# Start of a gated cross-attention and FFN kernel: loads reordered, Wq split by output columns, constant matmuls ahead of q, and new instruction orders

## The chip, the cores and the metric

The kernel runs on one core of one Trainium2 chip. The time is device microseconds of one launch, and the lower one is better. The names of the engines are those of the profile: PE is TensorE (matmul), PEld its weight load, DVE is VectorE, ACT ScalarE, POOL GpSimd, SP SyncE. SPq and ACTq in a row are the queues that issue DMAs.

## What is computed

A transformer layer over 8 batches of 256 tokens of width 512, with grouped cross-attention (32 query heads of 16, 8 key/value groups) and a gated FFN of width 1536:

```python
def xattn(X, enc, causal_mask, padding_mask, Wq, bq, Wk, bk, Wv, bv, Wo, bo):
    q, k, v = X @ Wq.T + bq, enc @ Wk.T + bk, enc @ Wv.T + bv
    # 8 groups, 4 query heads to a group, head size 16
    scores = einsum('bgrqd,bgkd->bgrqk', q, k) / sqrt(16)
    scores = where(causal_mask, -inf, scores); scores = where(padding_mask, -inf, scores)
    out = einsum('bgrqk,bgkd->bgrqd', softmax(scores), v)
    return out @ Wo.T + bo
def ffn(x, gate_w, up_w, down_w, gate_scale, up_scale, down_scale):   # weights rounded to fp8 e4m3
    return ((silu((x @ gate_w8) * gate_scale) * ((x @ up_w8) * up_scale)) @ down_w8) * down_scale
x = x + tanh(g_xattn) * xattn(layernorm(x), ctx_2048, ...)
x = x + tanh(g_ffn) * ffn(layernorm(x), ...)
```

## The kernel before

There is no loop over tiles. The work is cut into pieces with a name, a number n and a batch b, and five strings of words (PE_ORDER, ACT_ORDER, DVE_ORDER, POOL_ORDER, SP_ORDER) give the order of the pieces on each engine. `order()` turns a string into a list; the n-th word of a name is its n-th piece. Each engine walks through its list (the loops `for name, n, b in ..._ORDER`) and issues what belongs to the piece, with its semaphore waits, so a piece whose wait is not met holds up everything behind it on its engine. The strings were written out in advance; nothing is chosen at run time.

The pieces of one batch, in the order of the data:

- `load_x`, `stats1`, `power_0`, `shift1`, `norm1`: x comes in (`xin`), mean and variance on DVE, the power on POOL, the normalization on ACT (`xn`).
- `xT`: two pieces of four transposes on PE into a work bank; ACT copies the high half to f16 (`xh`) and DVE makes the rest (`xl`). Every product of activations is made of three f16 matmuls (high by high, high by low, low by high), so each weight has a high and a low part too.
- `q` (two pieces of 24 matmuls of 128x256), `k` (12) and `v` (24 of 128x128). `cT` makes the two f16 parts of the context on ACT and POOL (`ch`, `cl`).
- `put_q`, `get_q`, `put_k`, `get_k`: q and k go to DRAM and come back with the heads spread over the partitions (`qs`, `ks`). Each get is six DMAs.
- `maxima`: 16 pieces. PE makes the scores of four heads (4 matmuls), DVE takes the row maxima with the mask `mq` added (L741, four instructions of 0.42 us each, started 0.34 us apart). After eight of them `mrow` transposes the maxima, ACT and POOL split them, and `rows` writes them into `qs` as two more rows.
- `scores`: 16 pieces. For the first batch PE adds the mask by a matmul (`mask_b`, `ident_b`) and ACT exponentiates from the bank (`exp`); for later batches DVE adds the mask (L750).
- `weighted`, `sums`, `den`, `gather`, `recip`, `spread`, `split_att`, `out`: the weighted sum of v, its denominator, and the output projection.
- `norm2`, `x2T`, `gu` (12 pieces of 16 matmuls), `fuse`, `fsplit`, `down_a`, `down_b`, `add_y`, `store`: the FFN.

The weights are set up once. Each comes in as float32 into a buffer that is used for something else later (Wq into `un`, Wo into `ws`, Wk and Wv into `att_u`), ACT makes the high part and DVE the low part. This is the `setup` piece; SETUP names them in a fixed order, and the waits (`set_high`, `set_free`) count them in that order. The FFN weights come as 12 slabs of 768 KB through two staging buffers (`f_h`, `f_l`); the piece `slab` on SP issues the load and the piece `slab` on ACT waits for it and casts it to fp8 (L599). PE has three work banks, each given to the pieces in turn, and two pairs of banks for scores.

The first loads stand ahead of the lists. SP issues x, Wq (1 MB), ctx, Wo (1 MB), two masks, bv, two gates, spread, bo, the down scale and the padding rows; ACT issues ident, Wk, the columns of biases and scales, the padding columns and Wv.

## Time and profile before

| | us |
|---|---|
| median of 3 runs | 613.05 |
| the three runs | 613.05, 614.70, 609.72 |
| the profiled execution | 617.89 |
| its span, first to last instruction | 616.1 |
| PE busy | 563.3 (91%) |
| DVE busy | 485.9 (79%) |
| ACT busy | 363.7 (59%) |
| POOL busy | 255.8 (42%) |

The profiled execution took 1.8 us more than its span and 4.8 us more than the median. The page divides the span into 40 slices of 15.4 us and gives the busy tenths of each engine; the rows of a timeline give the start and the length of instructions, and in brackets how long the engine had been idle and what ended that.

### The profile page before, as it was taken

How to read it: one execution, taken by the hardware profiler on the slowest of the kernel's cores; microseconds unless marked ns; L12 is line 12 of the kernel's file. 1: busy time of each engine (PE TensorE's matmuls, PEld its weight loads, DVE VectorE, ACT ScalarE, POOL GpSimd, SP SyncE). 2: the span in 40 equal slices, each digit the busy share in tenths (PEclk: the TensorE clock that was granted, in tenths of full speed). 3: DMA queues.
4: the chain of work that ended last, by engine and by line, in shares of the span. 5: the costliest groups of instructions: out<-in, count | busy, mean ns of one | idle time of the engine just before them, and what ended most of it. 6: DMA issues, size and time to landing. Idle time of an engine off the chain costs nothing.

```text
span 616.1 us, 14167 instructions
## 1 busy us (share of the span) xinstructions
PE 563.3 (91%) x5056; PEld 348.4 (57%) x5056; DVE 485.9 (79%) x1505; ACT 363.7 (59%) x668; POOL 255.8 (42%) x339
## 2 busy tenths in 40 slices
PE   0846888799999999999999999999998999799997
PEld 0633343357754775467745765476645764376683
DVE  2377768999899889988999999988998898744321
ACT  3533675787754765556665576576644764475261
POOL 4043041123552078424464166306711464248274
PEclk9956999699999999999999999999997999799999
DMA  8662465571222033211322412112203000101000
GB/s 299 221 210 85 106 200 113 121 267 37 80 60 73 14 83 111 58 50 40 102 83 70 112 37 81 44 31 66 73 3 95 2 28 29 53 3 53 1 36 34
DMA packets 57158, 50.30 MB, mean 82 GB/s; under 512 B 8000, under 2 KB 46976, under 8 KB 57088
## 3 DMA queue, kind: packets, MB, share of 16 engines
q1 hardware_dynamic: 55600, 48.79, 26.9%
q8 instruction: 40, 0.66, 0.5%
q10 hardware_dynamic: 1488, 0.61, 0.4%
q14 instruction: 30, 0.25, 0.1%
HBM read 35.21 MB, written 9.44 MB: 72 GB/s over the span
## 4 chain that ended last, share of the span: by engine, by line
PE 73%; DVE 13%; issue 8%; POOL 2%; ACT 2%; DMA 1%; POOLq 0%; SPq 0%; DVEq 0%
PE work L982 25%; PE work L993 12%; PE av L890 8%; PE work L921 7%; PE work L960 5%; DVE junk L741 5%; PE sc L862 5%; PE sc L880 4%; DVE ws L750 2%; PE work L931 2%; DMA cin<-in_ctx_t 1%; PE work L907 1%; PE work L941 1%; PE sc L876 1%; PE work L969 1%
## 5 line engine op out<-in xcount | busy, mean ns | idle before, releaser
L741 DVE CUSTOM_DVE_ANT_0 junk<-sc,mq 128x256 bf16<-128x256 f32 x496 | 180.0, 418 | 26.5 <-PE sc L862 26.0
L750 DVE SCALAR_TENSOR_TENSOR ws<-sc,padc,mask_k 128x1024 f32<-128x1024 f32 x112 | 143.3, 1279 | 19.4 <-PE sc L880 18.0
L614 ACT ACTIVATE ws<-ws 128x1024 f32<-128x1024 f32 x112 | 116.8, 1053 | 19.7 <-DVE ws L750 19.4
L538 POOL TENSOR_TENSOR ff<-ga,up 128x256 f32<-128x256 f32 x96 | 69.3, 729 | 120.7 <-DVE ga L826 117.0
L982 PE MATMUL work<-h_h,wg 128*128 128x256 f16 x384 | 90.4, 276 | 0.0
L982 PE MATMUL work<-h_l,wg 128*128 128x256 f16 x384 | 89.8, 274 | 0.0
L982 PE MATMUL work<-h_h,wu 128*128 128x256 f16 x384 | 89.4, 273 | 0.0
L982 PE MATMUL work<-h_l,wu 128*128 128x256 f16 x384 | 89.3, 273 | 0.0
L674 ACT ACTIVATE up<-work,fuse_s 128x256 f32<-128x256 f32 x96 | 45.2, 471 | 55.5 <-PE work L982 55.5
L993 PE MATMUL work<-wd,f_h 128*128 128x512 fp8e4 x192 | 73.0, 380 | 0.1
L993 PE MATMUL work<-wd,f_l 128*128 128x512 fp8e4 x192 | 72.8, 379 | 0.0
L890 PE MATMUL av<-ws,va 128*32 128x256 f32 x1024 | 71.3, 397 | 1.5 <-ACT un L620 0.9
L545 POOL TENSOR_TENSOR f_l<-ff,f_h 128x256 f16<-128x256 f32 x96 | 63.5, 674 | 19.0 <-ACT f_h L682 18.9
L862 PE MATMUL sc<-ks,qs 48*128 48x256 f16 x512 | 52.5, 283 | 14.8 <-DVE mx L741 14.6
L826 DVE SCALAR_TENSOR_TENSOR ga<-th,work 128x256 f32<-128x256 f32 x96 | 38.8, 415 | 24.6 <-ACT th L675 24.3
L880 PE MATMUL sc<-qs,ks 50*128 50x256 f16 x512 | 51.7, 278 | 4.9 <-DVE ws L750 4.9
L620 ACT ACTIVATE un<-av 128x256 f32<-128x256 f32 x64 | 24.4, 381 | 48.5 <-PE av L890 48.1
L682 ACT ACTIVATE f_h<-ff 128x256 f16<-128x256 f32 x96 | 38.5, 416 | 21.1 <-POOL ff L538 21.0
L982 PEld LDWEIGHTS work<-h_h,wg 128*128 128x128 fp8e4 x384 | 37.6, 98 | 19.3 <-issue 15.0
L675 ACT ACTIVATE th<-work,tanh_s 128x256 f32<-128x256 f32 x96 | 45.1, 469 | 0.0
L890 PEld LDWEIGHTS av<-ws,va 128*32 128x32 f32 x1024 | 27.4, 111 | 29.6 <-issue 17.1
L741 DVE DVE_READ_ACCUMULATOR2_ANT mx<- 128x1 f32 x512 | 42.0, 82 | 0.0
(116 smaller groups left out, 1013.6 us busy)
## 6 DMA issues: line engine op xcount, KB each, us to landing
qs<-q_scratch SPq DMA_DIRECT2D x96, 64.0 KB, 2.4
xin<-in_x SPq DMA_DIRECT2D x8, 512.0 KB, 4.6
cin<-in_ctx_t SPq DMA_DIRECT2D x8, 512.0 KB, 4.5
xb<-in_x SPq DMA_DIRECT2D x8, 512.0 KB, 4.7
att_u<-un SPq DMA_DIRECT2D x128, 32.0 KB, 2.0
out_x<-yt SPq DMA_DIRECT2D x16, 256.0 KB, 2.2
ks<-k_scratch SPq DMA_DIRECT2D x48, 64.0 KB, 2.4
q_scratch<-qh SPq DMA_DIRECT2D x16, 128.0 KB, 2.5
```

Source lines behind the costliest of these rows:

```text
L538: pool.tensor_tensor(ff[:, n % RING, :], ga[:, n % RING, :], up[:, n % RING, :], ALU.mult).then_inc(ff_done, 1)
L545: pool.tensor_tensor(f_l[:, n, :], ff[:, n % RING, :], f_h[:, n, :], ALU.subtract).then_inc(fl_ready, 1)
L614: act.activation(ws[:, unit, :, :], ws[:, unit, :, :], ACT.Exp, scale=1.0 / SSC).then_inc(exp_done, 1)
L674: act.activation(up[:, n % RING, :], bank[:, L:2 * L], ACT.Copy, scale=fuse_s[:, n:n + 1])
L675: act.activation(th[:, n % RING, :], bank[:, 0:L], ACT.Tanh, scale=tanh_s[:, n:n + 1]).then_inc(tanh_done, 1)
L741: last = dve.tensor_tensor_reduce((junk, junk_1)[maxima_banks(n, b)][:, j, :], sc[maxima_banks(n, b)][:, place(j)], mq[b % 2][:, t, :], 1. ...
L750: dve.scalar_tensor_tensor(out=ws[:, n % 4, :, :], in0=sc[1][:, :].rearrange("p (j l) -> p j l", j=HPG), scalar=padc[b % 2][:, kt:kt + 1], ...
L862: last = mm(sc[maxima_banks(n, b)][:, place(j)], qs[b % 2][at:at + 3 * HD, pair, t * P:(t + 1) * P], ks[b % 2][at:at + 3 * HD, g, :], star ...
L880: last = mm(sc[1][:, place(j)], ks[b % 2][at:at + 3 * HD + 2, g, kt * P:(kt + 1) * P], qs[b % 2][at:at + 3 * HD + 2, pair, :], start=b >= ...
L890: last = mm(av[32 * j:32 * (j + 1), 0:L], va[b % 2][:, kt, n, :], ws[:, 2 * (n % 2) + kt, 2 * (j % 2) + j // 2, :], start=kt == 0, stop=kt ...
L982: last = mm(bank[:, L * i:L * (i + 1)], w[:, k, n * P:(n + 1) * P], d[:, k, :], start=k == 0 and s == 0, stop=k == KT - 1 and s == 1)
L993: last = mm(bank[:, :], d[:, c, n * P:(n + 1) * P], wd8[:, c, :], start=c == 0 and s == 0, stop=c == FT - 1 and s == 1)
```

## The change

1. Loads. x of the first batch is loaded in two halves, one from SP's queue and one from ACT's. Wq is loaded and set up by halves of its output columns (`wq_columns`) instead of halves of its input rows. Wo and the small loads go later on SP's queue, the padding rows earlier; Wk goes behind the padding columns on ACT's queue.
2. Setup. The words of the order strings name the weight, and each setup piece has its own semaphores, so they may stand in any order. The first `q` piece waits for `Wq0` alone, the second for `Wq1`.
3. The first `get_k` (batch 0) is issued by ACT instead of SP (`k_by_act=1`).
4. `warm`: 20 matmuls of 128x512 f16 on a constant tile into the bank `av`, 17 ahead of the first transposes and 3 behind them. They wait for one memset on DVE and nothing reads them.
5. `mask_b` is a piece of its own on POOL.
6. All five order strings are new.

```diff
-def order(words, setup=(), by_pe=0):
+def order(words, by_pe=0, k_by_act=0):
...
-            if name == "setup":
-                pieces.append((name, setup[k], 0))
+            if name in SETUP:
+                pieces.append(("setup", SETUP.index(name), 0))
...
 PE_ORDER = order("""
-    k xT*2 q*2 v xT*2 maxima*3 q maxima*6 mrow q maxima k maxima scores maxima scores xT maxima scores weighted
+    warm*17 xT*2 warm*3 q k q v xT*2 maxima*2 q maxima*2 q maxima k maxima*4 mrow v xT maxima*2 scores maxima scores
...
 ACT_ORDER = order("""
-    setup cT*2 setup*2 norm1 k xT*2 q setup*2 slab*2 gates setup q norm1 xT*2 cT q cT slab mrow norm1 q k exp*3 slab
+    slab Wk norm1 Wq0 xT*2 cT Wq1 cT q Wo0 k Wv gates q get_k norm1 xT*2 cT*2 slab norm1 slab q*2 Wo1 mrow k exp*2
...
 DVE_ORDER = order("""
-    setup stats1 setup shift1 setup*2 k xT*2 q setup v stats1 setup*2 q gates shift1 setup xT*2 maxima*8 q stats1
-    maxima shift1 maxima k maxima q maxima*4 v maxima xT maxima xT maxima*4 q maxima*3 stats1 maxima*2 shift1 q
+    stats1 shift1 Wq0 xT*2 mask columns Wk Wq1 q k stats1 gates shift1 Wo0 q Wv v xT*2 maxima*2 stats1 maxima shift1
+    maxima*5 q*2 maxima Wo1 k maxima*3 v maxima xT maxima*3 xT maxima*3 q maxima*4 stats1 maxima q maxima*3 k shift1
...
 SP_ORDER = order("""
-    load_c slab*2 load_x put_k put_q get_k get_q slab load_x put_q slab get_q slab put_q rows get_q put_k load_c
+    slab load_x slab put_q put_k load_c get_q load_x slab load_xb put_q get_q put_q rows put_k get_q load_c slab*2
...
+        def wq_columns(half):
+            return slice(2 * P * half, 2 * P * (half + 1))
...
+        def get_k(eng, b):
+            eng.wait_ge(k_out, 32 * (b + 1))
+            past(eng, t_ready, 16 * (b - 1))
+            if b < 2:
+                eng.wait_ge(sm_rows, 2)
+            for hf in range(2):
+                for s in range(3):
+                    src = k_dram[(0, 0, 1)[s]].rearrange("(g d) n -> d g n", d=HD)
+                    eng.dma_start(ks[b % 2][64 * hf + HD * s:64 * hf + HD * (s + 1), :, :], src).then_inc(ks_in, 16)
...
-            sp.dma_start(xin[:, :, :], x_v[0]).then_inc(ld_x, 16)
-            sp.dma_start(st_q[:, :, :], Wq_t.rearrange("(t p) i -> p t i", p=P)).then_inc(ld_wq, 16)
+            sp.dma_start(xin[:, 0, :], x_v[0][:, 0, :]).then_inc(ld_x, 16)
+            sp.dma_start(st_q[:, :, wq_columns(0)], wq_v[:, :, wq_columns(0)]).then_inc(ld_wq[0], 16)
             sp.dma_start(cin[:, :, :], c_v[0]).then_inc(ld_c, 16)
-            sp.dma_start(st_o[:, :, :], Wo_t.rearrange("(t p) i -> p t i", p=P)).then_inc(ld_wo, 16)
+            sp.dma_start(st_q[:, :, wq_columns(1)], wq_v[:, :, wq_columns(1)]).then_inc(ld_wq[1], 16)
...
+            act.dma_start(xin[:, 1, :], x_v[0][:, 1, :]).then_inc(ld_x, 16)
...
+            dve.memset(warm_in[:, :], 1.0).then_inc(warm_set, 1)
...
+            pe.wait_ge(warm_set, 1)
             for name, n, b in PE_ORDER:
+                if name == "warm":
+                    mm(av[:, :], warm_in[:, 0:P], warm_in[:, :], start=True, stop=True)
...
-                    if b == 0 and n == 0:
-                        pe.wait_ge(set_free, SETUP.index("Wq1") + 1)
+                    if b == 0:
+                        pe.wait_ge(set_free[f"Wq{n}"], 1)
```

On ACT, from its last first load on, before (in the names, `wk_h` and `wq_h` are the high parts of weights, `ch` that of the context, `xn` the normalized x, `wg` the fp8 gate weights):

```order
L590 ACT_TABLE_LOAD
L590 ACTIVATE wk_h<-att_u 128x512 [waits ld_wk]
L648 ACTIVATE ch<-cin 128x512 [waits ld_c] x2
L590 ACTIVATE wq_h<-un 128x1024 [waits ld_wq] x2
L626 ACTIVATE xn<-xin,nb,rs 128x512 [waits shift1]
L626 ACTIVATE xn<-xin,nb,rs 128x512
L654 ACTIVATE kh<-work,bk_c 128x256 [waits bank_ready0,columns_ready]
```

and now:

```order
L612 ACT_TABLE_LOAD
L612 ACTIVATE wg<-f_h 128x1536 [waits ld_f0]
L601 ACTIVATE wk_h<-att_u 128x512 [waits ld_wk]
L642 ACTIVATE xn<-xin,nb,rs 128x512 [waits shift1]
L642 ACTIVATE xn<-xin,nb,rs 128x512
L601 ACTIVATE wq_h<-un 128x4x256 [waits ld_wq0]
L653 ACTIVATE xh<-work 128x512 [waits bank_ready0]
L653 ACTIVATE xh<-work 128x512 [waits bank_ready1]
L666 ACTIVATE ch<-cin 128x512 [waits ld_c]
L601 ACTIVATE wq_h<-un 128x4x256 [waits ld_wq1]
L666 ACTIVATE ch<-cin 128x512 [waits ld_c]
```

The cast of the first slab, which stood behind the first q, is ACT's first piece, and the context and the second half of Wq stand behind the transposes.

On SP, the end of the first loads and what follows, before:

```order
L421 DMA dsb<-in_L_ffn_down_scale 128x512
L422 DMA padr_u<-in_mask_BxS_bk 128x2048
L438 DMA cin<-in_ctx_t 128x4x256 [waits c_low]
L432 DMA f_h<-in_L_ffn_gate_w 128x1536
L432 DMA f_l<-in_L_ffn_gate_w 128x1536
L435 DMA xin<-in_x 128x2x512 [waits normed1]
L461 DMA k_scratch<-kh 128x256 [waits bank_free0]
L461 DMA k_scratch<-kl 128x256
L447 DMA q_scratch<-qh 128x2x256 [waits bank_free0]
L447 DMA q_scratch<-ql 128x2x256
L470 DMA ks<-k_scratch 16x8x256 [waits sm_rows,k_out]
```

and now:

```order
L439 DMA dsb<-in_L_ffn_down_scale 128x512
L449 DMA f_h<-in_L_ffn_gate_w 128x1536
L452 DMA xin<-in_x 128x2x512 [waits normed1]
L449 DMA f_l<-in_L_ffn_gate_w 128x1536
L464 DMA q_scratch<-qh 128x2x256 [waits bank_free2]
L464 DMA q_scratch<-ql 128x2x256
L478 DMA k_scratch<-kh 128x256 [waits bank_free0]
L478 DMA k_scratch<-kl 128x256
L455 DMA cin<-in_ctx_t 128x4x256 [waits c_low]
L472 DMA qs<-q_scratch 16x8x256 [waits q_out0]
```

The first slab's load is the first issue behind the constants, the loads of ctx and of the second slab stand behind a wait, and `get_k` is gone from here.

On DVE, from the first `q` piece to the first maxima of the first batch, before:

```order
L772 SCALAR_TENSOR_TENSOR ql<-work,bq_c,qh 128x256 [waits q_high]
L772 SCALAR_TENSOR_TENSOR ql<-work,bq_c,qh 128x256
L718 SCALAR_TENSOR_TENSOR wv_l<-att_u,wv_h 128x512 [waits set_high]
L788 SCALAR_TENSOR_TENSOR va<-work,bv_b 128x8x16 [waits ld_bv,consts_pool,bank_ready2]
L788 SCALAR_TENSOR_TENSOR va<-work,bv_b 128x8x16
L688 BN_STATS bst<-xin 128x6 [waits ld_x]
L688 BN_STATS bst<-xin 128x6
L693 BN_AGGR mv<-bst 128x2 [waits stats1]
L693 BN_AGGR mv<-bst 128x2
L696 TENSOR_SCALAR ve<-mv 128x2 [waits bnagg1]
L702 TENSOR_SCALAR mask_q<-th 128x512 [waits ld_mask]
```

and now:

```order
L791 SCALAR_TENSOR_TENSOR ql<-work,bq_c,qh 128x256 [waits q_high]
L791 SCALAR_TENSOR_TENSOR ql<-work,bq_c,qh 128x256
L797 SCALAR_TENSOR_TENSOR kl<-work,bk_c,kh 128x256 [waits k_high]
L706 BN_STATS bst<-xin 128x6 [waits ld_x]
L706 BN_STATS bst<-xin 128x6
L711 BN_AGGR mv<-bst 128x2 [waits stats1]
L711 BN_AGGR mv<-bst 128x2
L714 TENSOR_SCALAR ve<-mv 128x2 [waits bnagg1]
L747 TENSOR_SCALAR tgbo<-tgbo,tg 128x512 [waits tanh_g]
L748 TENSOR_SCALAR tgo<-tg 128x1
L749 TENSOR_SCALAR dsb<-dsb,tg 128x512
L781 SCALAR_TENSOR_TENSOR nb<-mv,rs 128x2 [waits rstd1]
L736 SCALAR_TENSOR_TENSOR wo_l<-ws,wo_h 128x1024 [waits high_Wo0]
L791 SCALAR_TENSOR_TENSOR ql<-work,bq_c,qh 128x256 [waits q_high]
L791 SCALAR_TENSOR_TENSOR ql<-work,bq_c,qh 128x256
L736 SCALAR_TENSOR_TENSOR wv_l<-att_u,wv_h 128x512 [waits high_Wv]
```

The statistics of the second batch and, with them, the gates and `Wo0` stand ahead of the second q's low part, and `Wv`, which v waits for, stands behind it.

## Rows read from the trace of the kernel before

**Rows 1.** The page: the span in 40 slices of 15.4 us.

```profile
PE   0846888799999999999999999999998999799997
...
PEclk9956999699999999999999999999997999799999
```

**Rows 2.** Windows: stretch, its us, busy us by engine, granted clock, DMA share, GB/s.

```profile
3.00:14.00 11.00, 0.00 (x0) 0.00 (x0) 2.83 (x12) 4.94 (x6) 4.21 (x5) 1.00 1.05 358
...
40.00:63.90 23.90, 16.98 (x108) 9.51 (x104) 18.22 (x93) 6.71 (x12) 6.56 (x10) 0.65 0.41 138
63.90:100.00 36.10, 31.37 (x328) 15.05 (x332) 26.01 (x131) 26.72 (x36) 9.28 (x11) 1.00 0.50 137
100.00:121.80 21.80, 17.25 (x167) 8.09 (x166) 20.27 (x65) 13.61 (x19) 2.40 (x3) 0.77 0.57 127
...
520.00:540.00 20.00, 16.57 (x128) 8.15 (x126) 15.25 (x22) 10.02 (x17) 3.83 (x4) 0.83 0.14 41
```

**Rows 3.** Timeline of SP: start, duration, instruction.

```profile
11.21 0.43 SPq L422 DMA_DIRECT2D padr_u<-in_mask_BxS_bk  x1
...
28.31 2.80 SPq L470 DMA_DIRECT2D ks<-k_scratch  x6
```

**Rows 4.** DMA issues of 10 to 14.9 us: KB, us from issue to landing.

```profile
f_h<-in_L_ffn_gate_w SPq DMA_DIRECT2D x1, 768.0 KB, 7.3
...
padr_u<-in_mask_BxS_bk SPq DMA_DIRECT2D x1, 256.0 KB, 5.6
```

**Rows 5.** DMA issues of 46 to 60 us.

```profile
f_h<-in_L_ffn_up_w SPq DMA_DIRECT2D x1, 768.0 KB, 4.2
```

**Rows 6.** Timeline of ACT: start, duration, instruction, idle before and what ended it.

```profile
6.63 0.63 ACT L590 ACTIVATE wk_h<-att_u 128x512 f16<-128x512 f32 x1 [1.69 <-DMA att_u<-in_Wk_t]
...
14.90 1.52 ACT L626 ACTIVATE xn<-xin,nb,rs 128x512 f32<-128x512 f32 x2 [0.90 <-DVE nb L762]
...
18.62 0.60 ACT L637 ACTIVATE xh<-work 128x512 f16<-128x512 f32 x1 [0.26 <-PE work L907]
...
27.71 1.48 ACT L599 ACTIVATE wg<-f_h 128x1536 fp8e4<-128x1536 f32 x1
```

**Rows 7.** Timeline of PE, start of the program.

```profile
20.20 0.37 PE L921 MATMUL work<-xh,wq_h 128*128 128x256 f16 x1 [1.62 <-DVE xl L766]
...
26.49 0.27 PE L921 MATMUL work<-xl,wq_h 128*128 128x256 f16 x1
26.60 0.27 PE L921 MATMUL work<-xh,wq_l 128*128 128x256 f16 x1
...
37.39 1.97 PE L907 MATMUL work<-ident,xn 128*128 128x128 f32 x8 [7.54 <-ACT xn L626]
```

**Rows 8.** The chain that ended last, in order of time: start, us, what.

```profile
28.51 1.35 PE work L941 x24
...
55.51 5.03 PE work L921 x24
```

**Rows 9.** DMA issues of 27 to 31 us.

```profile
ks<-k_scratch SPq DMA_DIRECT2D x6, 64.0 KB, 2.5
...
q_scratch<-ql SPq DMA_DIRECT2D x1, 128.0 KB, 2.0
```

**Rows 10.** Timeline of DVE: setup work and maxima of the first batch.

```profile
14.79 2.35 DVE L718 SCALAR_TENSOR_TENSOR wq_l<-un,wq_h 128x1024 f16<-128x1024 f32 x2
...
30.30 1.27 DVE L688 BATCH_NORM_STATS2 bst<-xin 128x6 f32<-128x512 f32 x2
...
40.63 0.41 DVE L741 CUSTOM_DVE_ANT_0 junk<-sc,mq 128x256 bf16<-128x256 f32 x1
...
47.89 0.42 DVE L741 CUSTOM_DVE_ANT_0 x<-sc,mq 128x256 bf16<-128x256 f32 x1 [3.04 <-PE sc L862]
...
54.78 0.87 DVE L772 SCALAR_TENSOR_TENSOR ql<-work,bq_c,qh 128x256 f16<-128x256 f32 x2
```

**Rows 11.** Timeline of ACT, first exponential of the first batch.

```profile
63.92 1.11 ACT L610 ACTIVATE ws<-sc,padc 128x1024 f32<-128x1024 f32 x1 [1.12 <-PE sc L880]
```

More of the change, by code:

```diff
@@ new lines @@
+    weighted maxima scores maxima weighted x2T*2 maxima scores q maxima scores weighted gu maxima scores gu*2 scores
+    maxima k gu weighted maxima scores gu mrow gu scores maxima gu weighted scores maxima gu scores gu maxima scores
+    gu weighted maxima scores v gu scores maxima weighted gu down_a maxima scores down_a spread maxima scores
+    weighted spread down_b xT maxima scores xT down_b maxima scores mrow out maxima out weighted maxima scores q
+    scores weighted x2T maxima scores x2T q scores maxima weighted gu*2 maxima scores gu maxima gu scores maxima
@@ new lines @@
+    weighted gu*2 maxima scores mrow gu*2 k scores maxima weighted gu scores maxima gu weighted scores maxima gu
+    scores v gu scores weighted down_a scores maxima down_a spread scores maxima down_b spread maxima weighted xT
+    scores maxima down_b mrow xT maxima scores out*2 scores weighted maxima q maxima weighted scores x2T maxima x2T
+    q scores weighted maxima gu scores gu maxima scores gu*2 maxima scores gu weighted maxima scores gu mrow maxima
+    gu*2 weighted scores maxima gu k scores gu scores weighted maxima scores gu maxima weighted scores v gu maxima
@@ new lines @@
+    scores down_a spread down_a maxima scores spread down_b xT maxima scores weighted xT maxima down_b mrow maxima
+    scores out*2 weighted scores maxima q maxima weighted x2T*2 maxima scores q maxima gu scores gu scores maxima
+    weighted gu maxima scores k gu maxima scores weighted gu mrow maxima scores gu*2 scores maxima weighted gu*2
+    scores maxima v weighted scores gu scores maxima gu scores gu maxima scores weighted down_a maxima down_a spread
+    scores maxima down_b spread weighted maxima scores down_b mrow maxima scores out maxima out weighted xT scores
@@ new lines @@
+    maxima xT weighted scores k maxima x2T*2 q*2 maxima scores gu*2 maxima scores weighted gu maxima scores gu
+    maxima weighted scores gu mrow maxima scores gu weighted scores maxima gu*2 scores maxima gu weighted scores
+    maxima gu*2 maxima scores down_a gu maxima scores weighted down_a scores maxima spread down_b maxima scores
+    weighted spread down_b maxima scores mrow out scores out weighted maxima scores weighted v scores maxima x2T*2
+    maxima weighted scores gu maxima gu scores maxima gu scores gu maxima scores gu weighted maxima gu mrow scores
@@ L154 @@
     gu*12 down*2
[L155 removed]
+""", by_pe=BY_PE)
 POOL_ORDER = order("""
[L157 to L170 removed]
@@ L182 @@
+    load_xb rows load_c get_q put_q den gather put_k store get_k rows store load_x put_q load_c get_q load_xb gather
+    rows den put_q store get_q put_k gather get_k rows get_q put_k rows gather put_q load_xb den store get_q gather
+    store get_k rows load_xb gather put_q get_q rows store den store gather rows load_xb store gather den store
+    gather store*4
+""", k_by_act=1)
 IN_BANKS = ("xT", "q", "k", "v", "spread", "out", "x2T", "gu")
@@ L589, in _ @@
                     act.wait_ge(loaded, 16)
-                    act.activation(w_h, stage, ACT.Copy, scale=scale).then_inc(set_high, 1)
+                    act.activation(w_h, stage, ACT.Copy, scale=scale).then_inc(set_high[SETUP[n]], 1)
+                if name == "get_k":
+                    get_k(act, b)
                 if name == "gates":
@@ L616, in _ @@
                 if name == "sums":
+                    if n == 0 and b == 0:
+                        act.wait_ge(set_free["Wq1"], 1)
                     act.wait_ge(av_ready, AV_USE["weighted", n, b] + 1)
```

226 lines of the change are left out of this document (101 added, 125 removed).

## Prediction

> **What bounds the kernel now.** I read the slices first. PE shows 9 almost everywhere after the first tenth of the span, and the low digits lie in the first five slices, where PEclk is low too [rows 1]. So the long middle is bound by PE, an order with the same matmuls can win little there, and this change has to earn its time in the first 64 us. The windows put a size on it: from 40 to 63.9 us PE is busy 16.98 of 23.9 us at a mean clock of 0.65, and DVE 18.22; from 63.9 to 100 PE is busy 31.37 of 36.1 and DVE 26.01; from 100 to 121.8 DVE is busy 20.27 of 21.8 and PE 17.25, at 0.77 [rows 2]. Up to 100 us neither engine is full, they hand work to each other; then DVE binds until the FFN of the first batch gives PE its filler.
>
> The start is a chain: x, norm, xT, q, through DRAM and back, maxima. The reader should see four points of it: the transposes' second high part on ACT at 18.62 [rows 6], q at 20.20 [rows 7], the first maxima on DVE at 40.63 and the eighth's end at 54.78, where the next instruction begins [rows 10], the first exponential at 63.92 [rows 11]. These are what I compute anew.
>
> **The loads and the first piece of ACT.** ACT's list now begins with the cast of slab 0, ahead of Wk, norm1, Wq0 and xT. ACT works in order, so the whole start waits for that load. When does it land? SP reached the end of its first loads at 11.21 + 0.43 = 11.64 [rows 3]; one issue more (x in halves, Wq in halves, against one each, less one that ACT takes) makes about 12.1 for slab 0. The amount ahead of it is the same as before, and in that time the DMA engines were full: share 1.05, 358 GB/s from 3 to 14 us [rows 2]. The last of these loads landed at 11.21 + 5.6 = 16.8 [rows 3, 4]. Behind it 0.786 MB at 358 GB/s take 2.2 us: 19.0. The other way: slab 0 of the kernel before took 7.3 us from issue to landing in the same crowd [rows 4]: 12.1 + 7.3 = 19.4. Bounds: a slab in a quiet stretch took 4.2 us [rows 5], so 16.3 at the earliest; if the queue moves it only after everything and lands it a microsecond later, 20.5. I take L = 19.4. Before, ACT's first activation ran at 6.63 and norm1 at 14.90 [rows 6].
>
> **From L to the first maxima.** ACT: slab 1.4 (1.48 less the overlap that all rows show, 0.1), Wk 0.5, norm1 1.5 [rows 6]: the transposes begin at L+3.5. Before, eight transposes at the low clock kept PE 1.97 us [rows 7]. The second high part starts 1.9 us in, L+5.4; q started 1.6 us after that instruction (18.62 to 20.20) [rows 6, 7]: q at L+7.0. Wq0's low part (1.2 us, half of 2.35 [rows 10]) fits in between on DVE.
>
> The 17 constant matmuls are over by some 8 us and PE then has nothing until L+3.5 = 22.9. In this trace the clock was at its low level again after the 7.54 us without work ahead of 37.39 (eight transposes 1.97 us; the slices show it) [rows 1, 7]. So these 17 buy nothing; the three behind the transposes keep PE occupied for 1.3 us while it would wait. q began at 20.20 at the low clock, and only at 26.2 did the matmuls come 0.11 us apart (26.49, 26.60) [rows 7]; I let it rise as late in the unbroken stretch as there, 6.0 us, at L+9.5. Twelve matmuls at 0.21 (5.03 us for 24 [rows 8]) and twelve at 0.11: q ends at L+10.8. k (12 matmuls, 1.3) ends at L+12.1 and the second q (2.6) at L+14.7; Wk's and Wq1's low parts are ready at L+8.6 and L+9.7.
>
> The way out and back: the high part of q 0.9, low part 0.9, two puts issued by L+13.6, the second landing 2.0 after its issue at L+13.1 [rows 9], get_q 2.8 of issue (six ks copies took 2.80 [rows 3]) and 2.5 from the last issue to landing: L+20.1. k's parts reach DRAM at L+15.7; ACT issues get_k from there to L+18.5, in place by L+20.7. Here the change moves 2.8 us from SP onto ACT, and what is queued behind it on ACT is norm1 of batch 1, for which PE's list puts xT ahead of the maxima. Before, both gets stood one behind the other on SP, so the move saves up to 2.8 us there; with norm1 behind it, it gives back most: norm1 ends at L+20.1.
> The Trainium skill, DMA: Bandwidth & Descriptors, section "Issuing engines are not separate DMA queues", says that issuing on two engines saves only sequencer time, usually small beside the DMA. By that rule this part would be worth nothing, and the time 2.8 us later at most. The rows here speak against "small": 2.80 us of issue beside 2.5 to land [rows 3, 9].
>
> DVE in that stretch does stats1 (1.7 with the aggregate; 1.27 for the two statistics [rows 10]), gates 1.1, Wo0 1.2, the second q's low part 0.9 and only then Wv, at L+19.0; v, and so PE, waits for it from L+14.7. After 4.3 us idle I let the clock fall. v 2.6 at the low clock (1.35 at the full one [rows 8]), xT 1.97: the second high part at L+23.5, its low part 0.6 later, and the maxima on DVE another 0.6 later, L+24.8 = 44.2. With the clock kept it would be L+22.7. Before: 40.63. **The first maxima come 3.6 us later.**
>
> **From the maxima to the first exponential.** Before, eight maxima took 54.78 - 40.63 = 14.15 us for 8 x 1.38 = 11.0 of work; 3.04 was one wait for PE, which ran a whole q at the low clock between the third and the fourth [rows 10]. Now a q stands behind the second and one behind the fourth maxima, and stats1 (1.7) on DVE covers the first of them. If PE is at full clock by then (it has been busy since L+19.0), neither q (2.6) makes DVE wait: 11.0 + 1.8 = 12.8, and I take 13.2 for handovers. The eighth ends at 57.4, 2.6 later than before. Behind it DVE has both q low parts (1.6), one maxima (1.38), Wo1 (1.2), k (0.4), one maxima (1.38), 6.0 in all, and the eleventh maxima starts about 63.7 with the exponential 0.8 behind it: 64.5. Before: 63.92. The rows for the scores leave 2.8 us of issue and about 2 of landing after the split maxima, 64 as well, so they are level with it.
>
> So the start is nearly even in time: +0.6. But by then PE has done v of batch 1 and one xT of batch 2 beforehand, which stood behind the first scores: 1.35 [rows 8] and about 0.5. Against that, DVE had only one q low part (0.87, [rows 10]) more to do before. If PE binds the next stretch, the gain is 1.85 - 0.6 = 1.25; if DVE does, 0.87 - 0.6 = 0.3. Neither binds alone up to 100 us [rows 2]. I take 0.8.
>
> **The rest.** mask_b as a piece of its own, the per-weight semaphores and the column halves add no instruction in a place where someone waits; the work is the same. I find the same number of matmuls ahead of the first gu piece and of each later batch's in both lists, to within 2 us of work. The two dips of the middle and the end (520 to 540 us: PE busy 16.57 of 20, clock 0.83 [rows 2]) lie where batches change, and the new list has the same neighbours there. Nothing, with 3 us either way in the range.
>
> **Sum.** 616.1 - 0.8 = 615.3 for the span, 617.1 for a profiled execution with its 1.8 us around; that of before lay 4.8 over the median, so the median is forecast at 613.05 - 0.8 = 612.25, **612.2 us**, no change that a measurement can tell (1% of this kernel is 6.1 us, and its three runs spread over 5).
>
> **Rivals.** (a) The slab lands early, at 16.3. All points move 3.1 us forward: 609.1. For it: ACT's share of the loads leaves by its own queue. Against: 7.3 and 5.6 us in the rows of that stretch [rows 4].
> (b) The clock stays up from the constant matmuls, or rises at the third xT and stays. Then q(0) saves 1.2, and v and xT 2.1 on the path: about 609. Against: the idle 7.54 us and the low clock after it [rows 1, 7]. The Trainium skill, TensorE: Matmul & The Clock Gate, section "Why this matters for your kernels", advises to keep TensorE busy continuously to reach the full clock; it is the premise of the warm pieces, and by it alone they would pay.
> (c) The start isn't made up. If PE runs the two q pieces at the low clock (5.03 each [rows 8]), DVE waits 1.3 and 2.3 as it waited 3.04 [rows 10]; the distance from first maxima to first exponential stays 23.3 and the exponential comes at 67.5, 3.6 late: 616.6. It decides if PE's clock isn't up when the first q stands between maxima. If the later DVE-bound stretch then loses the clock once more than now (21.8 us with 17.25 busy at 0.77 [rows 2] is such a stretch, some 4 us lost), 621.
> (d) The new lists differ from the old ones in the long middle by chance: one of the later dips gone is 3.4 us, both 6.8: 605 to 609 with the forecast's start.
>
> **Chances.** Forecast 0.41 (own range 609 to 616), (a) and (b) together 0.22, of which a third with some of (d) below 607; (c) 0.23, of which 0.15 reaches 619; (d) 0.14. Below 606.9 lie 0.07 + 0.14 = 0.21, above 619.2 some 0.17, and 0.62 between. Range: 604 to 620.
>
> **What the profile after will show.** ACT's first activation is the slab cast, at about 19.4; if it is at 16, (a). Norm1 at 21.3, q at 26.4, first maxima on DVE at 44, first exponential at 64. The constant matmuls end by 9 us and PE is idle until 23. The forecast is wrong if ACT begins before 15 us, or if the middle (121 to 600 us) loses or gains over 3 us of PE time.

## The result and the profile after

The changed kernel took 620.94 us (median of 4 runs, 620.21 to 622.97), the kernel before 612.66 (4 runs, 609.72 to 614.70). The ratio is 1.0149, 95% interval 1.0116 to 1.0182: slower by 1.5%, 8.3 us. The forecast was 612.2 and its range ended at 620.0.

The slices of the page, 40 of 15.5 us, answer to [rows 1]:

```profile
PE   3557798788999999999999999999999999899997
...
PEclk8588599779999999999999999999999999899999
```

The reader is to see PEclk: in seven of the first ten slices it is below 9, against three before, and of the two late dips one is left, at 8 instead of 7. The first slices have to be read beside the matmuls, though: in the trace before, the column has 1.00 from 14 to 26 us, while the matmuls of 128x256 came 0.21 us apart from 14.16 to 26.1, the distance that they have in stretches with 0.50; so the low level lasted there until 26.1. PE's busy digits hardly tell the difference, since slow matmuls count as busy. The windows of the same stretches as [rows 2], with two more (14 to 26 and 58.7 to 75.8); the columns are the stretch, its length, the busy us of PE, PEld, DVE, ACT and POOL, the granted clock, the DMA share and GB/s:

```profile
3.00:14.00 11.00, 3.60 (x14) 1.33 (x12) 1.86 (x6) 1.28 (x1) 2.66 (x3) 0.86 1.08 355
14.00:26.00 12.00, 3.22 (x11) 2.01 (x11) 2.46 (x4) 6.27 (x9) 0.13 (x1) 0.50 0.51 181
40.00:63.90 23.90, 18.09 (x146) 13.08 (x144) 19.45 (x88) 10.17 (x17) 6.77 (x10) 0.79 0.52 136
58.70:75.80 17.10, 13.20 (x74) 5.77 (x74) 12.28 (x56) 4.83 (x7) 0.66 (x1) 0.50 0.55 183
63.90:100.00 36.10, 30.46 (x264) 12.15 (x260) 23.83 (x120) 21.85 (x29) 4.28 (x4) 0.83 0.54 173
100.00:121.80 21.80, 17.31 (x175) 8.19 (x174) 19.02 (x71) 13.99 (x18) 2.62 (x4) 0.84 0.18 46
520.00:540.00 20.00, 17.31 (x140) 7.17 (x133) 16.38 (x36) 11.55 (x17) 3.75 (x4) 0.92 0.18 55
```

From 14 to 26 us, where the kernel before ran k, transposed x and began q (PE busy 10.22 us in the same window of its trace), PE is busy 3.22 of 12 us. The row of 58.7 to 75.8 has a granted clock of 0.50, the lower of the two levels (1.2 GHz), for 17.1 us; in the trace before the same window has 0.95. The timeline of ACT answers to [rows 6]:

```profile
4.01 1.28 ACT L612 ACT_TABLE_LOAD   x1 [4.01 <-issue]
19.15 1.48 ACT L612 ACTIVATE wg<-f_h 128x1536 fp8e4<-128x1536 f32 x1 [13.86 <-DMA f_h<-in_L_ffn_gate_w]
20.54 0.61 ACT L601 ACTIVATE wk_h<-att_u 128x512 f16<-128x512 f32 x1
21.06 1.50 ACT L642 ACTIVATE xn<-xin,nb,rs 128x512 f32<-128x512 f32 x2
...
24.68 0.60 ACT L653 ACTIVATE xh<-work 128x512 f16<-128x512 f32 x1 [0.26 <-PE work L929]
...
36.01 2.76 ACTq L418 DMA_DIRECT2D ks<-k_scratch  x6
38.87 1.52 ACT L642 ACTIVATE xn<-xin,nb,rs 128x512 f32<-128x512 f32 x2 [3.99 <-issue]
...
68.10 1.11 ACT L624 ACTIVATE ws<-sc,padc 128x1024 f32<-128x1024 f32 x1 [7.22 <-PE sc L900]
```

ACT has nothing from 5.29 to 19.15: it waits for the load of slab 0 (`f_h`). Behind that stand the casts, norm1 at 21.06 and the second high part of xT at 24.68 (before 18.62). The timeline of SP and the DMA issues of 3 to 20 us say when that load was issued and how long it was on its way, as [rows 3] and [rows 4]:

```profile
9.12 0.43 SPq L439 DMA_DIRECT2D dsb<-in_L_ffn_down_scale  x1
9.74 0.33 SPq L449 DMA_DIRECT2D f_h<-in_L_ffn_gate_w  x1
```

```profile
f_h<-in_L_ffn_gate_w SPq DMA_DIRECT2D x1, 768.0 KB, 9.4
...
padr_u<-in_mask_BxS_bk SPq DMA_DIRECT2D x1, 256.0 KB, 8.2
```

Issued at 9.74, landed 9.4 us later: 19.1. The timeline of PE, as [rows 7]:

```profile
1.44 5.16 PE L872 MATMUL av<-warm_in 128*128 128x512 f16 x17 [1.44 <-DVE warm_in L739]
22.70 1.94 PE L929 MATMUL work<-ident,xn 128*128 128x128 f32 x8 [16.11 <-ACT xn L642]
24.44 1.49 PE L872 MATMUL av<-warm_in 128*128 128x512 f16 x3
26.15 0.37 PE L943 MATMUL work<-xh,wq_h 128*128 128x256 f16 x1 [0.23 <-DVE xl L785]
...
28.14 0.27 PE L943 MATMUL work<-xl,wq_h 128*128 128x256 f16 x1
...
38.17 0.23 PE L963 MATMUL work<-wv_h,ch 128*128 128x128 f16 x1 [4.22 <-DVE wv_l L736]
...
44.49 0.61 PE L882 MATMUL sc<-ks,qs 48*128 48x256 f16 x8 [2.30 <-DMA ks<-k_scratch]
...
69.27 1.03 PE L896 MATMUL sc<-mask_b,ident_b 128*128 128x512 bf16 x2 [0.52 <-ACT ws L624]
```

The 17 constant matmuls end at 6.6, and then PE waits 16.11 us. q starts at 26.15 at the low clock (0.21 us apart until 28.02, then 0.11). v waits 4.22 us for Wv's low part, the first maxima 2.30 us for `ks`. The DMA issues of 34 to 40 us have the gets, against [rows 9]:

```profile
cin<-in_ctx_t SPq DMA_DIRECT2D x1, 512.0 KB, 4.5
qs<-q_scratch SPq DMA_DIRECT2D x6, 64.0 KB, 5.1
ks<-k_scratch ACTq DMA_DIRECT2D x6, 64.0 KB, 5.8
```

The gets, issued side by side by SP and ACT, took 5.1 and 5.8 us from issue to landing, where `ks` took 2.5 before. 512 KB of ctx are issued just ahead, but that doesn't explain it alone: with both gets on SP and the same ctx ahead of them they took 3.1 and 2.8 us (below). The timeline of DVE, as [rows 10]:

```profile
25.92 1.40 DVE L720 TENSOR_SCALAR mask_q<-th 128x512 f32<-128x512 uint8 x1
...
27.57 1.12 DVE L725 TENSOR_SCALAR padc_all<-padc_u 128x16 f32<-128x16 uint8 x1
...
45.04 0.42 DVE L760 CUSTOM_DVE_ANT_0 junk<-sc,mq 128x256 bf16<-128x256 f32 x1 [1.39 <-PE sc L882]
...
47.80 1.28 DVE L706 BATCH_NORM_STATS2 bst<-xin 128x6 f32<-128x512 f32 x2
```

First maxima at 45.04 (before 40.63), first exponential at 68.10 (before 63.92, [rows 11]).

Both kernels were run and profiled a second time, and those two traces are the fairer pair, as told below. The legs between points of the program, in us (a batch's second norm is the first `x2n` row of that batch on ACT), each worked out as the difference of two starts:

| | before | before, 2nd | changed | changed, 2nd | slab later | combined |
|---|---|---|---|---|---|---|
| start to first maxima | 40.6 | 37.3 | 45.0 | 45.4 | 36.1 | 33.0 |
| to first exponential | 23.3 | 22.1 | 23.1 | 21.8 | 22.5 | 20.8 |
| to norm2 of batch 0 | 69.9 | 69.8 | 74.6 | 72.3 | 73.1 | 71.3 |
| to norm2 of batch 5 | 331.6 | 331.6 | 331.2 | 332.6 | 331.2 | 331.2 |
| to norm2 of batch 6 | 63.9 | 63.8 | 59.2 | 60.7 | 59.2 | 59.2 |
| to the end | 86.8 | 85.1 | 85.9 | 86.2 | 85.9 | 85.7 |
| span | 616.1 | 609.6 | 619.0 | 619.1 | 607.9 | 601.1 |

Second against second, the changed kernel loses 8.1 us up to the first maxima and 2.6 between exponential and norm2, and wins 3.0 between batches 5 and 6. The first trace of the kernel before is an unusual execution: of the 76 timed executions of that kernel on record here, 73 took 609.7 to 615.0 us and three took 617.7 to 617.9, this one among them.

### The profile page after: what moved, and what is told of

It is laid out like the page before. It is cut to its first block, busy times and chain, and to the rows that moved or that the text cites. A ratio compares the mean times of both kernels' runs of the same rounds, so it can differ in the third digit from the quotient of the medians.

```text
span 619.0 us, 14216 instructions
## 1 busy us (share of the span) xinstructions
PE 567.7 (92%) x5076; PEld 347.8 (56%) x5076; DVE 484.8 (78%) x1506; ACT 363.9 (59%) x668; POOL 255.8 (41%) x339
## 4 chain that ended last, share of the span: by engine, by line
PE 78%; DVE 9%; SPq 4%; DMA 4%; issue 2%; ACT 1%; ACTq 0%; POOLq 0%; POOL 0%; DVEq 0%
PE work L1005 28%; PE work L1016 12%; PE av L910 8%; PE work L983 7%; PE work L943 5%; PE sc L882 5%; PE sc L900 5%; DVE junk L760 4%; DMA ks<-k_scratch 2%; DMA f_h<-in_L_ffn_gate_w 2%; DVE ws L769 1%; PE work L963 1%; PE work L953 1%; PE sc L896 1%; PE work L929 1%
## 5 line engine op out<-in xcount | busy, mean ns | idle before, releaser
L769 DVE SCALAR_TENSOR_TENSOR ws<-sc,padc,mask_k 128x1024 f32<-128x1024 f32 x112 | 143.3, 1280 | 20.3 <-PE sc L900 17.9
L1005 PEld LDWEIGHTS work<-h_h,wg 128*128 128x128 fp8e4 x384 | 37.5, 98 | 19.1 <-issue 14.2
```

The costliest lines, as they stand in the source:

```text
L769: dve.scalar_tensor_tensor(out=ws[:, n % 4, :, :], in0=sc[1][:, :].rearrange("p (j l) -> p j l", j=HPG), scalar=padc[b % 2][:, kt:kt + 1], ...
L1005: last = mm(bank[:, L * i:L * (i + 1)], w[:, k, n * P:(n + 1) * P], d[:, k, :], start=k == 0 and s == 0, stop=k == KT - 1 and s == 1)
```

## The experiments

Ratios are to the kernel before, timed on the same chip beside each, with the 95% interval. Theory A: one word, the cast of slab 0 in first place on ACT, costs the time. The rivals put the loss on the new order further on, above all on PE at its low clock between the maxima, or on the constant matmuls.

**The slab's cast later.** The changed kernel with one word moved on ACT:

```diff
-    slab Wk norm1 Wq0 xT*2 cT Wq1 cT q Wo0 k Wv gates q get_k norm1
+    Wk norm1 Wq0 xT*2 cT Wq1 cT q Wo0 k Wv slab gates q get_k norm1
```

> The changed kernel with one word moved: the cast of slab 0 on ACT goes from the first place to behind Wv. Theory A (the 13.9 us for which ACT waits for slab 0 are what the start loses): ACT begins with Wk near 8 to 9 us, q at about 15 instead of 26.2, first maxima on DVE at 34 to 36 instead of 45.0, and the time falls by 8 to 11 us, to 610 to 613. Theory B (other waits, such as the late Wv and the low clock, take the place of the stall): q comes 10 us earlier, but the time falls by less than 4 us.

Measured: 610.10 us, ratio 0.9961 (0.9931 to 0.9991), 10.8 under the changed kernel (9.7 under its second set of runs, 619.83). With the word moved, the rest of the change is 2.1 us faster than the kernel before. The timeline of ACT in it:

```profile
10.82 0.63 ACT L601 ACTIVATE wk_h<-att_u 128x512 f16<-128x512 f32 x1 [5.51 <-DMA att_u<-in_Wk_t]
11.35 1.50 ACT L642 ACTIVATE xn<-xin,nb,rs 128x512 f32<-128x512 f32 x2
...
14.98 0.60 ACT L653 ACTIVATE xh<-work 128x512 f16<-128x512 f32 x1 [0.26 <-PE work L929]
```

norm1 starts at 11.35 instead of 21.06, 9.7 us sooner, and the median follows by 9.7 to 10.8. Now norm1 waits for Wk, whose load ends the idle time ahead of 10.82.

**The same word put into the kernel before.** Its slab cast goes first on ACT, its load ahead of ctx on SP:

```diff
-    setup cT*2 setup*2 norm1 k xT*2 q setup*2 slab*2 gates      (ACT)
+    slab setup cT*2 setup*2 norm1 k xT*2 q setup*2 slab gates
-    load_c slab*2 load_x put_k                                  (SP)
+    slab load_c slab load_x put_k
```

> The kernel before with the cast of slab 0 as ACT's first piece, and its load ahead of the second ctx on SP, nothing else. Theory A: ACT begins at 19 to 20 instead of 6.6 us, norm1 at 24 instead of 14.9, and the time rises by 9 to 12 us over the kernel before, so the stall alone costs more than the whole change. Theory B (there is slack elsewhere in the start): it rises by less than 5 us.

Measured: 623.67 us, ratio 1.0174 (1.0123 to 1.0225), 11.4 us over the kernel before beside it (612.23). The timeline of ACT in it:

```profile
20.14 1.48 ACT L599 ACTIVATE wg<-f_h 128x1536 fp8e4<-128x1536 f32 x1 [15.40 <-DMA f_h<-in_L_ffn_gate_w]
...
25.97 1.52 ACT L626 ACTIVATE xn<-xin,nb,rs 128x512 f32<-128x512 f32 x2 [0.89 <-DVE nb L762]
```

The cast waits 15.40 us for the same load, and the old order pays for it as the new one does. Two words were moved here, the cast and its load. So slab 0 in first place costs 10 to 11 us in either order.

**Without the constant matmuls,** the changed kernel with `warm*17` and `warm*3` taken out of PE's list:

> The changed kernel without its 20 constant matmuls. Theory A (PE is idle for 16 us between them and the transposes, so they buy nothing): within 1.5 us of the changed kernel, q at 26 us as before. Rival (the three behind the transposes bring the clock up early): q ends 1 to 2 us later and the time rises by as much.

Measured: 619.64 us, 1.0127 (1.0086 to 1.0168), q at 26.46 against 26.15. The medians differ by 1.3 us, in favour of the version without them, and the intervals overlap: they buy nothing here.

**The same, with the slab later:**

> The slab cast moved and the 20 constant matmuls ahead of q taken out. With the slab cast moved, PE is idle for 5.2 us between the 17 of them and the transposes. Theory (the matmuls pay once the stall is gone: q ran at full clock from 17.2 us on): 2 to 3 us slower than with them. Rival (q isn't what the start waits for): within 1 us.

Measured: 609.16 us, 0.9936 (0.9909 to 0.9963), 0.9 under the version with them. I expected them to be worth 2 to 3 us once the long wait was gone; they weren't, though q's matmuls, 0.11 us apart from 16.95 on with them, came 0.21 us apart up to 19.35 without.

**Constant matmuls put into the kernel before,** 28 ahead of k and 4 behind the first transposes:

```diff
-    k xT*2 q*2 v xT*2 maxima*3 q
+    warm*28 k xT*2 warm*4 q*2 v xT*2 maxima*3 q
```

> The kernel before with constant matmuls of 128x512 on PE, 28 ahead of k and 4 behind the first transposes, nothing else. In its two profiles the clock rose at 26.2 and at about 18 us, and the first maxima on DVE followed at 40.6 and 37.3. Theory (the time at which the clock rises varies between executions, and q at half clock costs the start 3 us): the clock is high before q in the profile, first maxima at 36 to 37.5, and the median falls by 0 to 2 us with less spread. Rival (it makes no difference to the median): within 0.5 us.

Measured: 611.30 us, 0.9977 (0.9954 to 1.0000). q ran at 19.42 at the full clock, first maxima at 36.94 as expected, and the median moved 1.2 us, at the edge of what can be told. The spread didn't shrink as I had expected (609.24 to 614.25, against 609.77 to 614.76), so the clock ahead of q is not what spreads the usual executions. Its trace is a control for the first one of the kernel before: all legs from the first maxima on are the same (23.3, 69.9, 331.6, 63.9, 86.8), and only the first is shorter, 36.9 instead of 40.6. So about 3.7 us of that trace are the low clock up to 26.2 us, in k, the transposes and q.

**Constant matmuls between the maxima.** The changed kernel with 18 more, which keep PE at work while it waits for DVE; `hold` waits until DVE has taken the eighth maxima and writes a score bank that is free then:

```diff
-    maxima k maxima*4 mrow v xT maxima*2 scores
+    maxima k maxima*2 warm*5 maxima warm*4 maxima warm*3 mrow v xT maxima hold*6 maxima scores
...
+                if name == "hold":
+                    pe.wait_ge(m_free, UNITS // 2)
+                    mm(sc[1][:, 0:D], warm_in[:, 0:P], warm_in[:, :], start=True, stop=True)
```

> The changed kernel with 18 more constant matmuls of 128x512, which stand where PE waits for DVE among the maxima of the first batch (5 before the eighth, 4 before the ninth, 3 before mrow, 6 before the eleventh, these into the second score bank). In the changed kernel the clock is low from 58.7 to 75.8 us. Theory C (that low stretch costs about 4 us of the start): the clock stays high there and the time falls by 3 to 5 us. Rival (DVE sets the pace there): the clock is high, the time within 1 us.

Measured: 619.06 us, 1.0114 (1.0068 to 1.0159). One window of it, to be held against the same window of the changed kernel above:

```profile
58.70:75.80 17.10, 12.68 (x114) 5.15 (x113) 15.10 (x72) 6.43 (x9) 0.67 (x1) 1.00 0.48 167
```

The clock stays at 1.00 instead of 0.50, and the leg from the exponential to norm2 is 70.2 us instead of 74.6. In the second trace of the changed kernel the same window has 0.62 and the leg is 72.3. In the median 1.9 us appear (0.8 against the second set of runs), where I had expected 3 to 5 and which is less than the intervals can separate.

**The same fill with the slab later:**

> The kernel with the slab cast moved, and with the 18 constant matmuls among the first maxima as well. The clock was low from 58.2 to 71.9 us with the slab cast moved alone. Theory C (the gaps that the new list leaves on PE ahead of mrow let the clock fall, and the first scores then run at half of it, whatever ACT waited for): 3 to 5 us less than the slab cast moved alone, 605 to 607. Rival: within 1 us of it.

Measured: 609.08 us, 0.9922 (0.9898 to 0.9946), 1.0 under the version without fill, where I had expected 3 to 5. Here the fill didn't hold the clock all the way: it was at 0.50 from about 61 to 68 us, against 58 to 71 without, and the leg from the exponential to norm2 is 71.6 us against 73.1.

**Wv's low part ahead of stats1 on DVE,** with the slab later:

```diff
-    Wk Wq1 q k stats1 gates shift1 Wo0 q Wv v
+    Wk Wq1 q k Wv stats1 gates shift1 Wo0 q v
```

> The slab cast moved, and on DVE the low part of Wv ahead of the second batch's statistics instead of behind the second q, so that PE doesn't wait 4.0 us for it ahead of v. Theory (that wait, and the clock that falls in it, is on the path): v and xT end 3 us earlier, but the first maxima wait for k from DRAM (2.2 us of that wait is seen), so the time falls by 0.5 to 2 us. Rival: the gain is 3 us or more, since the clock stays up.

Measured: 608.58 us, 0.9932 (0.9908 to 0.9957), 1.5 less than with the slab later alone. It did not hold up in the combined version (below).

**The first get_k back on SP,** with the slab later:

```diff
-    slab gates q get_k norm1                  (ACT)
+    slab gates q norm1
-    put_q put_k load_c get_q                  (SP)
+    put_q put_k load_c get_k get_q
```

> The slab cast moved and the first get_k issued by SP again, ahead of get_q. Theory (both gets one behind the other on SP cost 2.8 us, of which norm1 on ACT, 2.8 us earlier, gives some back): q arrives 2.8 us later, and the time rises by 0 to 2 us. Rival: no difference, within 0.5 us.

Measured: 608.38 us, 0.9918 (0.9891 to 0.9944), 1.7 less, where I had expected up to 2 more. First maxima 33.90 against 36.07, of which 1.07 is Wk landing earlier in that execution (9.75 against 10.82). q did not arrive 2.8 us later: one behind the other on SP the gets took 3.1 (`ks`) and 2.8 us (`qs`) to land, where side by side from SP and ACT, with the slab later too, they took 5.8 and 5.1. From the first get's issue to the first maxima it is 8.46 us (25.44 to 33.90) instead of 9.86 (26.21 to 36.07). So issuing from two engines saved nothing in these traces, one of each; the intervals of the two medians overlap.

**Both kernels again, unchanged:**

> The kernel before, unchanged, for a second profile. Its first profile took 4.8 us over the median and had PE's clock low around 466 to 473 and 531 to 538 us. Theory (these two low stretches belong to the old lists): both are there again, and the sixth to seventh norm2 lie 63 to 64 us apart. Rival (they come and go from execution to execution): one of them is gone, and the distance is about 60 us, as in the new lists.

> The changed kernel, unchanged, for a second profile. Theory (the points of its start are fixed by the slab's landing): ACT begins at 19 to 20 us, first exponential of the first batch at 67 to 69, first norm2 at 140 to 143; time 619 to 622. Rival: the start moves by over 2 us from execution to execution.

Measured: 612.02 us, 0.9997 (0.9975 to 1.0018), and 619.83, 1.0120 (1.0075 to 1.0166). Both theories held: the old lists have both late dips and 63.8 us between the norms again, and the points of the changed kernel's start came back (slab cast at 19.29, first exponential at 67.23; the first norm2 at 139.56 is 0.4 early). The second trace of the kernel before has, on PE, DVE and ACT in turn:

```profile
19.73 0.27 PE L921 MATMUL work<-xh,wq_h 128*128 128x256 f16 x1 [1.61 <-DVE xl L766]
19.83 0.27 PE L921 MATMUL work<-xl,wq_h 128*128 128x256 f16 x1
```

```profile
37.26 0.41 DVE L741 CUSTOM_DVE_ANT_0 junk<-sc,mq 128x256 bf16<-128x256 f32 x1
```

```profile
59.40 1.11 ACT L610 ACTIVATE ws<-sc,padc 128x1024 f32<-128x1024 f32 x1 [1.13 <-PE sc L880]
```

q runs at the full clock from its first matmul (0.27 us, the next 0.10 later), where in [rows 7] it took 0.37 and the clock rose only at 26.2. First maxima and first exponential are 3.4 and 4.5 us earlier than in [rows 10, 11]. The two spans differ by 6.5 us; 1.7 of the rest lie behind norm2 of batch 6.

**Combined:** slab later, Wk behind the transposes so that norm1 doesn't wait for it, get_k on SP, and the 18 fill matmuls.

```diff
-    slab Wk norm1 Wq0 xT*2 cT Wq1 cT q Wo0 k Wv gates q get_k norm1
+    norm1 Wq0 xT*2 Wk cT Wq1 cT q Wo0 k Wv slab gates q norm1
```

> The slab cast behind Wv, the high part of Wk behind the transposes (norm1 waited for Wk's landing at 10.8 us though its own inputs were there at 8.3), the first get_k on SP, and the 18 matmuls among the first maxima. Theory (the four add up as far as they lie on the chain of the start): norm1 at 8.4 instead of 11.35, first norm2 at 125 to 128, time 603 to 606. Rival (batch 0 and 1 are bound by DVE up to norm2, and what comes earlier waits there): 607 to 609.

Measured: **603.93 us**, ratio 0.9859 (0.9820 to 0.9897), better than both kernels, and within the 603 to 606 that I expected. norm1 at 8.51, first maxima at 32.96. What each of the four gives in it was tried for two only, the fill and the slab (below). The timeline of ACT in it:

```profile
8.51 1.52 ACT L642 ACTIVATE xn<-xin,nb,rs 128x512 f32<-128x512 f32 x2 [3.23 <-DVE nb L781]
...
10.88 1.06 ACT L653 ACTIVATE xh<-work 128x512 f16<-128x512 f32 x2
```

**Combined, and Wv early:**

> The same as the combined kernel with the low part of Wv ahead of the second batch's statistics as well. Theory: PE no longer waits some 4 us for it, and 0.5 to 1.5 us less than the combined kernel. Rival: no difference, since the first maxima wait for k and q from DRAM.

Measured: 606.51 us, 0.9896 (0.9855 to 0.9937), 2.6 more rather than 0.5 to 1.5 less, with intervals that overlap. So Wv early is worth nothing that I can show; in both of these traces PE waits for `qs` ahead of the first maxima.

**Combined without the fill:**

> The combined kernel without the 18 matmuls among the first maxima. Theory C (low clock in the first scores makes the way from the first exponential to the first norm2 longer): the clock is low again for over 10 us around the first scores, that way is 73 to 75 us instead of 71.3, and the median rises by 1.5 to 3 us. Rival: within 1 us of the combined kernel.

Measured: 606.21 us, 0.9900 (0.9874 to 0.9926), 2.3 more. The two windows, of the version without fill and of the one with it:

```profile
53.00:72.00 19.00, 16.71 (x103) 4.82 (x104) 10.98 (x57) 9.16 (x13) 1.15 (x1) 0.58 0.60 169
```

```profile
53.00:72.00 19.00, 16.07 (x145) 5.85 (x144) 14.20 (x73) 11.78 (x17) 4.29 (x4) 0.91 0.55 169
```

Here 19 us run at a clock of 0.58 without the fill and at 0.91 with it; DVE gets 14.20 us of work done instead of 10.98. The leg from the exponential to norm2 is 74.7 us without and 71.3 with it, as expected. The three pairs with and without fill give 1.9 (0.8 by the second set of runs), 1.0 and 2.3 us, all of one sign; the intervals of each pair overlap, so the size is only roughly known.

**Combined with the slab first again:**

> The combined kernel with the cast of slab 0 as ACT's first piece again. Theory A (the stall is passed on in full, whatever else is mended): ACT begins at 19 to 20 us instead of 8.5, and the time rises by 9 to 12 us over the combined kernel. Rival (part of it is made up): by less than 7 us.

Measured: 618.75 us, 1.0092 (1.0059 to 1.0125), 14.8 over the combined version, where I had expected 9 to 12. The timeline of ACT in it:

```profile
20.53 1.48 ACT L612 ACTIVATE wg<-f_h 128x1536 fp8e4<-128x1536 f32 x1 [15.22 <-DMA f_h<-in_L_ffn_gate_w]
21.92 1.50 ACT L642 ACTIVATE xn<-xin,nb,rs 128x512 f32<-128x512 f32 x2
```

norm1 is at 21.92 against 8.51, so 13.4 us later, and the end 15.9 in the span.

## Why the prediction was wrong

**What bounds the kernel, and where the change acts: right.** The middle (norm2 of batch 0 to batch 5) is 331 to 333 us in every version; the net loss lies ahead of it.

**The loads and ACT's first piece: right.** L was forecast at 19.4 and is 19.15, norm1 21.3 and is 21.06. Of the two ways to L, the one by the bytes ahead (19.0) holds; the one that gave 19.4 came out by luck, since the slab was issued at 9.74, not 12.1, and took 9.4 us, not 7.3. q was forecast at 26.4 and is 26.15, the first maxima at 44.2 and are at 45.04. The 0.8 between is a term that was mis-sized: I let `ks` land 2.5 us after its issue, at 40.1, with 4 us in hand; it took 5.8, started a little later too, and PE waited 2.30 for it. The constant matmuls bought nothing, as said. That ACT's wait for slab 0 is what the change costs is shown in both directions: without the word -10.8 us, with it in the old order +11.4, in the combined version +14.8. The forecast's error is to have let later pieces make this wait up.

**First failed step, the baseline of the sum.** "Before: 40.63" and "Before: 63.92" come from one execution, 4.8 us over the median, in which q ran at the low clock. I took differences against it and put them on the median. In the second trace, 611.47 us and so near the median, the points are 37.26 and 59.40: the change costs about 8 us up to the first maxima (45.04 and 45.39 against 37.26), not 3.6. Of the miss 4.5 us come from here, about 3.7 of them by the low clock up to 26.2 us (the trace with constant matmuls in the kernel before). I had the sign of it in hand (profile 617.89, median 613.05) and did not ask where in the trace the 4.8 us lay.

**Second failed step, "From the maxima to the first exponential".** I forecast 20.3 us (44.2 to 64.5); it took 23.1 and 21.8. I had argued that nothing would wait for PE because its clock would be up. Instead the eight maxima took 14.1 us (45.04 to 59.12) against my 13.2. Behind them PE, with short pieces and waits for DVE, went to the low clock at 58.7, and the way from the eighth maxima to the exponential took 9.0 us against my 7.1: DVE waited 0.66 and 0.82 us for PE ahead of the tenth and the eleventh maxima, the mask's matmuls took 1.03 us for two, and ACT waited 7.22 us for the scores. (The sum there had a slip too: 57.4 and 6.0 make 63.4, not 63.7.) Rival (c) gave the time, an exponential at 67.5 (68.10 and 67.23 came), but by luck: it had both q pieces at the low clock and DVE waiting 3.6 us for them within the eight maxima. In the trace the first q (45.03 to 49.4) had its matmuls 0.21 us apart only up to 48.4, the second q ran at the full clock, and DVE's waits there are 0.9 us in all. Its 621 is luck as well: the further loss that it put between 100 and 121.8 us didn't come (granted clock 0.84 there, 0.77 before). Of the miss 2.7 us are this step, by the second trace (67.23 against 64.5).

**Third failed step, the credit of 0.8.** v and xT done beforehand were to shorten the stretch behind the exponential: the forecast has it 1.4 us shorter, the 0.8 gained and the 0.6 by which the exponential was to be late. PE did have less to do in it, but it took longer. The lines of PE in that stretch, first exponential to norm2, grouped; the kernel before (second trace):

```profile
L890 PE MATMUL av<-ws,va 128*32 128x256 f32 x176 | 13.5, 430 | 0.2 <-ACT un L620 0.2
...
L876 PE MATMUL sc<-mask_b,ident_b 128*128 128x512 bf16 x30 | 9.0, 383 | 2.0 <-ACT ws L610 2.0
...
L941 PE MATMUL work<-wv_h,ch 128*128 128x128 f16 x16 | 2.8, 220 | 0.0
```

and the changed kernel (second trace):

```profile
L910 PE MATMUL av<-ws,va 128*32 128x256 f32 x176 | 14.2, 449 | 0.1
L896 PE MATMUL sc<-mask_b,ident_b 128*128 128x512 bf16 x30 | 10.8, 447 | 2.8 <-ACT ws L624 2.8
...
L963 PE MATMUL work<-wv_h,cl 128*128 128x128 f16 x8 | 2.5, 314 | 0.0
```

There are 8 v matmuls of each kind instead of 16, but each takes 314 ns against 219, and one of the mask 447 against 383. In all, PE is busy 63.34 us with 548 matmuls at a clock of 0.84, against 59.68 with 580 at 0.93. The leg grew by 2.6 us instead of shrinking by 1.4: 4.0 us of the miss. That the clock is the reason is shown for the leg, in one trace each: with the fill matmuls it is 70.2 instead of 74.6 and 72.3 (changed), 71.6 instead of 73.1 (slab later), 71.3 instead of 74.7 (combined). In the medians no single pair is clear of the noise.

**"The rest: nothing": off by a gain.** The new lists take 59.2 to 60.7 us from norm2 of batch 5 to batch 6, the old ones 63.8 and 63.9 (62.5 with the slab first). The first pair of traces gains 4.7 us here, more than the 3 us that the prediction allowed the middle, the second pair 3.0. The dip of the old lists at 466 to 473 us (granted clock 0.54 in the first trace) is not there in the changed kernel (1.00 in both). That was part of rival (d). Which of the reordered pieces does it was not tried.

Together, second trace against second: +8.1 at the maxima, -0.3 to the exponential, +2.6 to norm2, +1.0 in the middle, -3.0 between batches 5 and 6, +1.1 to the end: +9.5 in the span, 7.8 in the medians. Against the forecast of -0.8 the spans miss by 10.3: 4.5 from the baseline, 2.7 to the exponential, 4.0 to norm2, -0.9 behind it. The medians miss by 8.7; the 1.6 between the two come from taking single executions for their medians and stay unassigned. The wait named for the start was right, the claim that it is made up was not; the rival that said so had 0.23, and by the right baseline it should have been the forecast.

**get_k on ACT** was forecast to save up to 2.8 us and give most back; it costs about 1.7 (or nothing, by the intervals). The price named, norm1 of batch 1 behind it on ACT, was paid (the row of 38.87), but held PE up little: xT of batch 1 waited 0.21 us for it in the changed kernel's second trace and 0.18 in the one with the slab later. What went wrong is the landing: 5.8 and 5.1 us side by side instead of 3.1 and 2.8 one behind the other.

## What to carry to other kernels

An engine that works in order must not begin with a piece whose load stands at the end of the queue: 1.4 us of work in first place cost 10 to 15 us, since the whole start waits with it. Put there the piece whose input comes first, and check this for each word, as Wk ahead of norm1 was the same fault in small (11.35 against 8.51). And before taking differences against a trace, see where it stands to the median and look at a second one: here the reference points of the start differed by 3.4 and 4.5 us between two executions, about half of what the change did.
